# Adding the tap count to the gap inside PSUM, with products on 32-row strips

## What is computed

```python
freq  = MIN_FREQ + sigmoid(wave[..., 0]) * (MAX_FREQ - MIN_FREQ)      # 1 to 16
phase = tanh(wave[..., 1]) * freq
offs  = phase[..., None] + freq[..., None] * taps                    # 32 taps, -15.5 to 15.5
pos   = clip(l + offs, 0.0, 511)
i0    = floor(pos); frac = pos - i0
gathered = x[i0] + frac * (x[min(i0 + 1, 511)] - x[i0])
bins  = clip(floor((offs + 256) / 512 * 64), 0, 63)                  # which of 64 weights
y     = sum over taps of kmat[bins] * gathered
```

## Time and profile before

| what | value |
|---|---|
| median of 3 runs (lowest, highest) | 1351.81 us (1351.02, 1352.03) |
| span of the profiled execution | 1350.9 us |
| median of the runs less that span | 0.9 us |
| mean granted TensorE clock, share of full | 0.957 |
| busy over the span: TensorE, VectorE, ScalarE, GpSimd | 1145.0, 1037.5, 932.5, 707.9 us |

### The profile page before, as it was taken

How to read it: one execution, slowest core, us unless ns; L and a number is a source line. 1 busy time by engine, 2 the same in 40 slices (tenths; PEclk the granted TensorE clock), 3 DMA queues, 4 the chain that set the end, 5 groups by cost and what they waited for, 6 DMA issues and landing times.

```text
span 1350.9 us, 34980 instructions
## 1 busy us (share of the span) xinstructions
PE 1145.0 (85%) x11343; PEld 780.0 (58%) x11343; DVE 1037.5 (77%) x2316; ACT 932.5 (69%) x1906; POOL 707.9 (52%) x903
## 2 busy tenths in 40 slices
PE   4699989998998999899899989999931999999840
PEld 2366656666665666666566666666620665656520
DVE  4699999899999999999999999999942333333336
ACT  2588887888888788888888887888800555555520
POOL 5344167458457745845774584554436454555520
PEclk9899999999999999999999999999965999999975
DMA  6646455445655654554554456454512452222236
GB/s 207 164 122 178 105 148 159 125 123 174 145 133 149 159 135 121 165 153 121 159 151 141 123 147 153 131 153 118 155 61 63 115 156 72 72 72 70 68 142 253
DMA packets 213184, 181.13 MB, mean 134 GB/s; under 512 B 147600, under 2 KB 183184, under 8 KB 212112
## 3 DMA queue, kind: packets, MB, share of 16 engines
q1 hardware_dynamic: 204336, 160.99, 43.7%
q0 software_dynamic: 8672, 17.92, 3.9%
HBM read 96.73 MB, written 82.12 MB: 132 GB/s over the span
## 4 chain that ended last, share of the span: by engine, by line
PE 60%; DVE 11%; issue 9%; POOL 9%; ACT 5%; DMA 4%; SPq 1%; DVEq 0%; POOLq 0%; ACTq 0%
PE ps L1003 12%; PE ps L1147 8%; PE ps L1023 7%; PE ps L990 6%; PE ps L995 5%; DVE aw L1310 5%; PE ps L1162 4%; PE ps L1010 3%; PE ps L954 2%; PE ps L1033 2%; PE ps L1045 2%; PE ps L1154 2%; DMA att<-y_scratch 2%; ACT ee L783 2%; POOL slot_scratch L577 2%
## 5 line engine op out<-in xcount | busy, mean ns | idle before, releaser
L783 ACT ACTIVATE ee<-ps,f 128x512 f32<-128x512 f32 x512 | 354.3, 692 | 115.5 <-PE ps L990 111.2
L1310 DVE TENSOR_TENSOR aw<-dq,ks 128x520 f32<-128x520 int32 x512 | 416.8, 814 | 3.2 <-DMA ks<-k_scratch 3.2
L1300 DVE SCALAR_TENSOR_TENSOR dq<-ps,ee 128x512 int32<-128x512 f32 x512 | 349.9, 683 | 42.4 <-PE ps L995 39.1
L1003 PE MATMUL ps<-ident,aw 128*128 128x128 f32 x2048 | 314.6, 276 | 36.8 <-ACT att L791 19.9
L1003 PEld LDWEIGHTS ps<-ident,aw 128*128 128x128 f32 x2048 | 239.1, 141 | 180.4 <-DVE aw L1310 67.3
L791 ACT ACTIVATE att<-ps 128x512 f32<-128x512 f32 x512 | 310.0, 606 | 20.1 <-PE ps L1003 18.7
L995 PE MATMUL ps<-cn,ptt 128*128 128x512 bf16 x512 | 195.1, 381 | 10.0 <-DVE dq L1300 9.5
L608 POOL COPY kn<-kn 128x256 f32<-128x256 f32 x64 | 25.4, 396 | 337.4 <-DVE kn L1290 332.4
L711 POOL DMA_INDIRECT y_scratch<-aw,idu x135 | 129.2, 957 | 130.2 <-ACT aw L874 129.0
L990 PE MATMUL ps<-cp,ptt 128*128 128x512 bf16 x512 | 197.1, 385 | 0.0
L577 POOL DMA_INDIRECT slot_scratch<-hrow,spotu x128 | 141.4, 1105 | 44.6 <-issue 33.4
(11 more groups left out here) (177 smaller groups left out, 1689.7 us busy)
## 6 DMA issues: line engine op xcount, KB each, us to landing
k_scratch<-kn SPq DMA_DIRECT2D x64, 512.0 KB, 3.6
ka<-e_scratch SPq DMA_DIRECT2D x64, 512.0 KB, 3.3
ks<-k_scratch SPq DMA_DIRECT2D x128, 130.0 KB
e_scratch<-kr SPq DMA_DIRECT2D x128, 126.0 KB, 3.8
dl<-slot_scratch SPq DMA_DIRECT2D x135, 65.0 KB, 1.9
att<-y_scratch SPq DMA_DIRECT2D x16, 512.0 KB, 5.3
xc<-in_x SPq DMA_DIRECT2D x8, 512.0 KB, 6.5
h_scratch<-hx SPq DMA_DIRECT2D x16, 256.0 KB, 4.2
```

The lines of the kernel that those rows point to most:

```text
L783: act.activation(ee[:, T % ERING, :], ps_p[T % 2][:, :], ACT.Relu, scale=f27[:, i % 2, r, h:h + 1]).then_inc(s_e, 1)
L1003: last = nc.tensor.transpose(bank[:, j * P:j * P + P], aw[:, T % RING, o:o + P], ident[:, :])
L1300: nc.vector.scalar_tensor_tensor(dq[:, T % DRING, o:o + 512], ps_n[T % 2][:, :], SCALE, ee[:, T % ERING, :], ALU.mult, ALU.add).then_inc(s ...
L1310: nc.vector.tensor_tensor(aw[:, T % RING, :].rearrange("p (g k) -> p g k", k=8), dq[:, T % DRING, :].rearrange("p (g k) -> p g k", k=8), r ...
```

## The change

It has these parts.
- **The sum in PSUM.** The gap product, its Relu and the sum live in one bank of a ring of four (`ps_s`, `BANKS`), in place of two rings of two. ScalarE's Relu reads and writes that bank. TensorE then adds the count product onto it, without clearing. The rings `ee` and `dq` and the function `counted` go.
- **The upper clamp by absorption.** The count is added in two products: first one with terms near 2^90, in which everything that should be clamped is lost by rounding, then one ("undo") that takes those terms away again. So a tile has three products of 512 columns instead of two.
- **The lower clamp** goes into the weighting, as a max with -32 x SCALE on half-shifted counts; the edge counts get the shift in `edge_terms`, and `ends` sets one end column instead of two.
- **Residue order.** The 512 columns are ordered by residue, then by group: the weight of a column is then `ks[..., o:]` over 64 neighbouring columns, repeated for each residue. The weighting reads PSUM, and for r > 0 takes two instructions (residues below r, and from r). `dt` has the same order, so that the transposes read without a shift.
- **Strips.** The parameters and the constants of a tile are taken on the 32 rows of its head alone, partitions 32 (T % 4) on, with contraction 32 instead of 128; `cn` and `cp` are smaller.
- **Lookahead.** Gap and ramp are issued 3 tiles ahead (was 4), the count products 1 ahead (was 3). The gap product waits for the weighting of the tile that had the bank before, the count product for the ramp.

```diff
-NX = 8 * NG
-DRING = 3
-AHEAD = 3
-ERING = 4
+BANKS = 4
+GATE = 2.0 ** 90
...
-        cn = sb("cn", [P, QUAD, 512], bf16)
-        cp = sb("cp", [P, QUAD, 512], bf16)
+        cn = sb("cn", [P, 2, 512], bf16)
+        cp = sb("cp", [P, 512], bf16)
...
-        ps_n, ps_p, ps_t, ps_y, side = ps[0:2], ps[2:4], ps[4:6], ps[6], ps[7]
+        ps_s, ps_t, ps_y, side = ps[0:BANKS], ps[4:6], ps[6], ps[7]
...
             def h_steps(i):
...
-                pool.tensor_tensor(rows(dt[:, 0, 0:1], [[RES, P], [1, RES - 1]]), rows(ht[:, q, 0, 0:1], [[1, P], [P, RES - 1]]),
-                                   rows(ht[:, q, 1, 0:1], [[1, P], [P, RES - 1]]), ALU.subtract)
+                pool.tensor_tensor(dt[:, :, 0:RES - 1, :].rearrange("p b r t -> p r b t"), ht[:, q, 0:RES - 1, :].rearrange("p r (b t) -> p r b t", b=2),
+                                   ht[:, q, 1:RES, :].rearrange("p r (b t) -> p r b t", b=2), ALU.subtract)
...
             def ends(R):
...
-                pool.tensor_scalar(ka[:, R % 2, :, 0], k[:, :, LO], 16 * SCALE, None, ALU.mult)
-                pool.tensor_scalar(ka[:, R % 2, :, PADK - 1], k[:, :, LO + BINS - 1], 16 * SCALE, None, ALU.mult).then_inc(s_kf, 1)
+                pool.tensor_scalar(ka[:, R % 2, :, 0], k[:, :, LO], TAPS * SCALE, None, ALU.mult).then_inc(s_kf, 1)
...
-            pool.memset(dq[:, :, :], 0)
...
-                if T >= ERING:
-                    act.wait_ge(s_dq, T - ERING + 1)
-                act.activation(ee[:, T % ERING, :], ps_p[T % 2][:, :], ACT.Relu, scale=f27[:, i % 2, r, h:h + 1]).then_inc(s_e, 1)
+                act.activation(ps_s[T % BANKS][:, :], ps_s[T % BANKS][:, :], ACT.Relu, scale=f27[:, i % 2, r, h:h + 1]).then_inc(s_e, 1)
...
-                if T + ERING < NT:
-                    gap(T + ERING)
+                if T + BANKS - 1 < NT:
+                    gap(T + BANKS - 1)
...
+            def strip(T):
+
+                k = ROWS * (T % QUAD)
+                return slice(k, k + ROWS), ptt[k:k + ROWS, T // TILES % 2, 2 * (T // HEADS % RES) + T % HEADS // QUAD, :]
 
             def gap_on(T):
-                if T >= 2:
-                    pe.wait_ge(s_e, T - 1)
-                nc.tensor.matmul(ps_p[T % 2][:, :], params_of(T), cp[:, T % QUAD, :], start=True, stop=True).then_inc(s_p, 1)
+                if T >= BANKS:
+                    pe.wait_ge(s_aw, T - BANKS + 1)
+                at, params = strip(T)
+                nc.tensor.matmul(ps_s[T % BANKS][:, :], params, cp[at, :], start=True, stop=True).then_inc(s_p, 1)
 
             def tile_on(T):
-                if T >= 2:
-                    pe.wait_ge(s_dq, T - 1)
-                nc.tensor.matmul(ps_n[T % 2][:, :], params_of(T), cn[:, T % QUAD, :], start=True, stop=True).then_inc(s_n, 1)
+                pe.wait_ge(s_e, T + 1)
+                at, params = strip(T)
+                nc.tensor.matmul(ps_s[T % BANKS][:, :], params, cn[at, 0, :], start=False, stop=False, skip_group_check=True)
+                nc.tensor.matmul(ps_s[T % BANKS][:, :], params, cn[at, 1, :], start=False, stop=True, skip_group_check=True).then_inc(s_n, 1)
...
-                    o = RES - r + j * P
-                    last = nc.tensor.transpose(bank[:, j * P:j * P + P], aw[:, T % RING, o:o + P], ident[:, :])
+                    last = nc.tensor.transpose(bank[:, j * P:j * P + P], aw[:, T % RING, j * P:j * P + P], ident[:, :])
...
-                if T + ERING < NT:
-                    gap_on(T + ERING)
-                if T + AHEAD < NT:
-                    tile_on(T + AHEAD)
+                if T + BANKS - 1 < NT:
+                    gap_on(T + BANKS - 1)
+                if T + 1 < NT:
+                    tile_on(T + 1)
                 turn_tile(T)
...
-            def counted(T):
-
-                o = RES - T // HEADS % RES
-                dve.wait_ge(s_n, T + 1)
-                dve.wait_ge(s_e, T + 1)
-                if T >= DRING:
-                    dve.wait_ge(s_aw, T - DRING + 1)
-                nc.vector.scalar_tensor_tensor(dq[:, T % DRING, o:o + 512], ps_n[T % 2][:, :], SCALE, ee[:, T % ERING, :], ALU.mult, ALU.add).then_inc(s_dq, 1)
-
             def weighted(T):
...
-                dve.wait_ge(s_dq, T + 1)
+                dve.wait_ge(s_n, T + 1)
                 if T >= RING:
                     dve.wait_ge(s_at, UNIT["tile", T - RING] + 1)
-                nc.vector.tensor_tensor(aw[:, T % RING, :].rearrange("p (g k) -> p g k", k=8), dq[:, T % DRING, :].rearrange("p (g k) -> p g k", k=8),
-                                        rows(ks[:, R % 2, h, 0:1], [[1, NG], [0, 8]]), ALU.mult).then_inc(s_aw, 1)
+                src = ps_s[T % BANKS][:, :].rearrange("p (q g) -> p q g", g=HP)
+                dst = aw[:, T % RING, :].rearrange("p (q g) -> p q g", g=HP)
+                for a, b, o in ((0, r, 0), (r, RES, 1)):
+                    if a < b:
+                        ins = nc.vector.scalar_tensor_tensor(dst[:, a:b, :], src[:, a:b, :], -TAPS * SCALE,
+                                                             rows(ks[:, R % 2, h, o:o + 1], [[0, b - a], [1, HP]]), ALU.max, ALU.mult)
+                ins.then_inc(s_aw, 1)
...
-                nc.vector.tensor_tensor(kr[:, R % 2, :], en[:, R % 2, :], kd[:, R % 2, :], ALU.mult).then_inc(s_kr, 1)
+                nc.vector.scalar_tensor_tensor(kr[:, R % 2, :], en[:, R % 2, :], -TAPS / 2 * SCALE, kd[:, R % 2, :], ALU.add, ALU.mult).then_inc(s_kr, 1)
```

More of the change, by code:

```diff
@@ L158, in build @@
         ht = sb("ht", [P, 2, RES, P])
-        dt = sb("dt", [P, 2, L])
+        dt = sb("dt", [P, 2, RES, HP])
         dl = sb("dl", [P, 2, NJ, HEADS, 2 * D])
@@ L175, in build @@
         ks = sb("ks", [P, 2, HEADS, NG])
-        ee = sb("ee", [P, ERING, 512])
-        dq = sb("dq", [P, DRING, NX], i32)
-        aw = sb("aw", [P, RING, NX])
+        ee = sb("ee", [P, 2, 512])
+        aw = sb("aw", [P, RING, 512])
         att = sb("att", [P, SLOTS, 512])
@@ L225, in build @@
         stage = att[:, :, :].rearrange("p a n -> p (a n)")
-        stages = [stage[:, 0:QUAD * 512], stage[:, QUAD * 512:2 * QUAD * 512], stage[:, 2 * QUAD * 512:2 * QUAD * 512 + QUAD * EDGES]]
+        stages = [stage[:, 0:1024], stage[:, 1024:1536], stage[:, 1536:1536 + QUAD * EDGES]]
         zeros = flat[:, QUAD * 512:QUAD * 512 + KALL]
@@ L500, in _ @@
             pool.memset(middle[:, :], MIN_FREQ + (MAX_FREQ - MIN_FREQ) / 2)
[L501 to L504, removed]
+            pool.memset(pt[:, :, 26:ROWS], 0.0)
+            pool.memset(pt[:, :, 9:13], 1.0)
+            pool.memset(pt[:, :, 22:26], 1.0)
+            pool.memset(dt[:, :, RES - 1, HP - 1], 0.0)
             pool.memset(both[:, :, :], 0.0)
@@ L631, in _ @@
             pool.wait_ge(s_stage[1], 16)
[L632 removed]
+            pool.tensor_copy(cp[:, :], stages[1]).then_inc(s_cast, 1)
             pool.wait_ge(s_stage[2], 16)
@@ L813, in _ @@
             counted(0)
-            for T in range(ERING):
+            for T in range(BANKS - 1):
                 gap(T)
@@ L971, in steps_turned @@
                 for j in range(NJ):
-                    last = nc.tensor.transpose(bank[:, j * P:j * P + P], dt[:, b, j * P:j * P + P], ident[:, :])
+                    last = nc.tensor.transpose(bank[:, j * P:j * P + P], dt[:, b, 2 * j:2 * j + 2, :].rearrange("p q t -> p (q t)"), ident[:, :])
                 last.then_inc(s_at, 1)
@@ L1075, in _ @@
             counts(0)
-            for T in range(2):
+            for T in range(BANKS - 1):
                 gap_on(T)
-            for T in range(2):
-                tile_on(T)
-            gap_on(2)
-            tile_on(2)
-            gap_on(3)
+            tile_on(0)
             for b in range(2):
@@ L1499 @@
     magic, eta = 1.5 * 2 ** 23, 2.0 ** -20
-    m = np.arange(512) - 256
+    m = (np.arange(HP)[None, :] * RES + np.arange(RES)[:, None]).reshape(512) - 256
     one = np.ones(512)
@@ L1503 @@
     count = np.zeros((ROWS, 512))
+    undo = np.zeros((ROWS, 512))
     gap = np.zeros((ROWS, 512))
     ends = np.zeros((ROWS, EDGES))
+    reach = 1024
     for k in range(3):
-        count[3 * k:3 * k + 3] = [m, -one, -one]
+        for a, sign in ((count, 1), (undo, -1)):
+            a[3 * k:3 * k + 3] = sign * GATE / reach * np.stack([m, -one, -one])
+        count[13 + 3 * k:16 + 3 * k] = SCALE * np.stack([m, -one, -one])
         gap[3 * k:3 * k + 3] = [-m, one, one]
-        gap[12 + 3 * k:15 + 3 * k] = [m + 1, -one, -one]
+        gap[13 + 3 * k:16 + 3 * k] = [m + 1, -one, -one]
         ends[3 * k:3 * k + 3] = [edge, 0 * edge, 0 * edge - 1]
-    for a, sign in ((count, 1), (gap, -1), (ends, 1)):
+    for a, sign in ((count, 1), (undo, -1)):
+        a[9], a[10] = sign * GATE / reach * (reach - TAPS) / 2, sign * GATE / reach / 2
+        a[11], a[12] = sign * GATE * magic, -sign * GATE * magic
+    count[22], count[23], count[24], count[25] = -SCALE * eta, SCALE * magic, -SCALE * magic, -SCALE * TAPS / 2
+    for a, sign in ((gap, -1), (ends, 1)):
```

(4 more changed lines are left out.)

16 lines of the change are left out of this document (5 added, 11 removed).

## The result

The changed kernel takes 1409.55 us (median of 4 runs, 1408.87 to 1411.69) against 1351.41 (1350.83 to 1352.03) for the kernel before on the same chip: ratio 1.0436, 95% interval 1.0421 to 1.045, **58 us slower**. Forecast were 1423 us and a loss of 72, with the range 1385 to 1530. The sign, the mechanism and the range hold; the loss is 13.5 us smaller than worked out.

The account below looks back on a forecast made before the run. VectorE was taken to bound the kernel, TensorE next. TensorE's work +0.24 and waits -0.10 gave +0.14 us a tile, times 512 = +72 us, less 1: 1422 against the profiled span, 1423 against the runs' median; range 1385 to 1530.

Parts of the forecast that it names:

- VectorE bounds, TensorE is next: Tile loop before the change: VectorE 93% busy; TensorE's own work 1.66 of 1.835 us a tile, only 10% behind.
- VectorE's new pass: Weighting from PSUM, two instructions where r > 0: 415 us in all, bounds 350 and 480, replacing two passes of 767 us.
- The third product: TensorE, each tile: one more product of 512 columns, the undo, adds 0.22 us.
- Entering strips: TensorE, full array to row strips: 0.10 us a change, new for 5 of 8 tiles, +0.06 a tile; bounds 0 and 0.10.
- Leaving strips: TensorE, before the four transposes of every tile: +0.15 us; bounds 0 and 0.15.
- Overlap: TensorE, gap and count products on different strips: 0.03 left of the gap product's 0.22, -0.19 us a tile; bounds -0.21 and 0.
- The sum: TensorE's terms per tile together: +0.24 us, bringing TensorE to 1.90 us a tile.
- Waits: TensorE's waits in the loop fall from 0.17 to 0.07 us a tile; bounds 0.03 and 0.14.
- the first (no overlap): Rival: entering strips costs something but gap and count stay serial, 97 us more, 1520 us; chance 0.17.
- the second (strips free): Rival: entering and leaving row strips costs nothing while they overlap, 28 us saved, 1323 us; chance 0.20.
- The fourth: Rival: lookahead of one decides; VectorE's pair or ScalarE's write longer by 0.2 makes half the tiles late, 1474 us; chance 0.05.
- The third: Rival: row strips bring neither cost nor overlap; +0.22 - 0.10 a tile, 61 us, 1413 us; chance 0.06.

Follow-up runs that it names:

- full_noundo: The changed kernel with its products on the full 128-row array and without the undo product, upper clamp left out (output differs): 1335.1 us.
- one_pass: The changed kernel with one weighting instruction a tile in place of two, residues below r weighted with the neighbouring bin (output differs): 1406.9 us.
- ahead2: The changed kernel with the count and undo products issued two tiles ahead instead of one: 1404.9 us.
- pair: The changed kernel, full output, with the strip products of two tiles issued together in every second step: 1297.5 us, ratio 0.9597 to the kernel before.
- pair_ramps: The kernel pair with ScalarE's two ramps done together in the odd step, ahead of its eviction: 1306.7 us.
- noundo: The changed kernel on strips without the undo product and the 2^90 terms of the count, upper clamp left out (output differs): 1325.0 us.

## Why the prediction came out right, and where its size was off

- **VectorE bounds, TensorE is next.** Half right. TensorE's own 1.66 of 1.835 is 1.658 by the count. That 0.13 of the 0.17 goes with VectorE's load was too much: full_noundo has the same work on TensorE, 325 us less on VectorE, and gains 0.034 a tile. The forecast did not suffer, since with the longer TensorE step the waits fell as far as it said.
- **VectorE's new pass**, 415 us: 381.7. That is 28 us more than the 512 single instructions of one_pass, 0.06 for each of the 448 second ones, where 0.15 was taken for a start. Above the lower bound of 350, off the path.
- **ScalarE's write to PSUM**, 0.69: 0.669, between the bounds. Nothing hung on it.
- **The third product**, +0.22: 0.226. Right.
- **Entering strips**, +0.06 (0.10 at 5 of 8 tiles): 205 against 109 ns. Right.
- **Leaving strips**, +0.15: 0.090 in front of the transposes and, as a mean over the tiles, 0.038 within them, 0.128. Too much by 0.02.
- **Overlap**, -0.19 with 0.03 left of the gap product: 3 ns are left, -0.212, the lower bound. The 0.03 was read from narrow column strips, 32 matmuls in 1.01 us, as the spacing averaged over a group. Too little gain by 0.02.
- **The sum**, +0.24: the pieces as measured make 0.226 + 0.06 + 0.128 - 0.212 = 0.20, and the count without the slow stretches gives +0.200. **This is the sum that was mis-sized**, by the two terms before it, leaving and overlap: 0.04 x 512 = 20 us too much.
- **Waits**, from 0.17 to 0.07: 0.172 to 0.057 at full clock. Near in size, by luck in its reasons. The forecast kept 0.07 for GpSimd's end terms and ScalarE's evictions, and let VectorE's weighting be late only once a pair. Of the 0.057, nearly all stands in front of the transposes, and of the 27 us between undo and transposes from tile 64 on 18 fall on four of the 64 tiles of a pair (heads 3 and 5 of residues 1 and 2). The view of the transposes' line (for whom its engine stood idle, us, times) names the weighting:

```profile
  DVE aw L1296: 71.7, 103
  ACT att L783: 6.1, 14
```

- **The clock** had no term. It cost 12 us.
- **GpSimd and SP**, nothing or 1 us: first transposes at 41.2 against 41.9 us.

So the forecast missed by 20 us too much work and 8 us too few waits saved, and 12 us of slow clock that it did not know of hid part of that. On the clock of the kernel before, the time would have been near 1397 us, still in the range but 26 below the forecast; that the miss is only 13.5 us is luck. The prediction also called the pieces of the chain start-to-start; they run from end to end, which leaves sums over whole steps as they are. Of the rivals, the first (no overlap) and the second (strips free) each had half of the fact against it: gap and count overlap fully, and going in and out costs 0.19 a tile together. The fourth is refuted by ahead2 and one_pass. The third gave 1413, nearer to the time than the forecast, by neither cost nor overlap; the spacings refute it as a mechanism, but the two nearly cancel, so that its sum comes close.

## What to carry to other kernels

Row strips and other tiling modes are paid for by the number of changes between them and full-array work: one product saved by overlap a tile was worth about the two changes around it, and only grouping the strip work of two tiles made strips win. Taking work from the busiest engine by giving the next one a product more needs the second engine's slack, here 10%, and not the first one's load: count what the receiver's step becomes before what the giver saves. When two kernels differ by under 1% and the work and waits do not say why, look at the granted clock over short windows: a mean of 0.98 against 1.00 was about the whole difference between strips and full array here.

## What the runs showed that was not expected

- The second matmul on another row strip, into another bank, starts 3 ns behind the first, 512 columns notwithstanding, and four of them start within 17 ns (pair).
- In pair the gap product that stands behind both undo products in the program has its start recorded 0.21 us ahead of theirs (305.07 against 305.28): its strip was free, theirs were taken by the counts.
- The first float32 transposes after strips are usually 165 and not 109 ns apart, once, in the changed kernel and in pair alike.
- In the loop (tiles 64 to 511) the clock fell to 1.2 GHz 9, 8, 7, 7, 6, 4, 1 and 0 times in the eight kernels with row strips, and 0, 0, 0 and 1 times in the four on the full array. So strips alone do not bring it about (pair_ramps has them and no fall), and what does was not found.
- A shorter step gives its waits back: in noundo and full_noundo 0.07 to 0.08 a tile returned as soon as the undo product was gone, with VectorE no more than 59% busy in the loop (noundo, windows view below) and ScalarE 84%:

```profile
43.00:950.00 907.00, 847.20 (x9894) 555.87 (x9893) 534.84 (x1651) 760.46 (x1471) 405.15 (x615) 0.99 0.54 146
```

Neither engine is full, and 0.14 us a tile of waits stay, for VectorE's weighting more than for ScalarE. That points at when their work comes and not at how much it is; no run showed which order would be better.
